# A gated delta-rule block with a 4-bit feed-forward: decay exponents from differences of running sums in bf16 pieces, filler products removed, steps reordered

## The reference

```python
gk = -jnp.exp(A_log) * jax.nn.softplus(hidden_states @ Wgk + dt_bias)
beta = jax.nn.sigmoid(hidden_states @ Wb + b_b)
def step(S, inp):
    qt, kt, vt, bt, gt = inp
    S = S * jnp.exp(gt)[..., None, None]
    kv = jnp.einsum('bhk,bhkv->bhv', kt, S)
    delta = (vt - kv) * bt[..., None]
    S = S + jnp.einsum('bhk,bhv->bhkv', kt, delta)
    ot = jnp.einsum('bhk,bhkv->bhv', qt, S)
    return (S, ot)
```

## Time and profile before

| what | value |
|---|---|
| time, median of 3 runs | 2731.93 us (2730.82 to 2735.35) |
| the profiled execution, its own time | 2730.7 us |
| its span | 2728.9 us |
| busy PE, DVE, ACT, POOL | 2608.6, 2389.7, 2259.6, 1628.3 us |
| mean granted clock of PE | 0.984 of full |

### The profile page before, as it was taken

The page is one execution under the profiler, slowest core; times in us unless marked ns, Lnnn a source line. Parts: engine busy times, 40 slices in busy tenths (PEclk is TensorE's granted clock), DMA queues, the critical chain, the costliest instruction groups (busy, mean ns, idle before and its releaser), DMA issues.

```text
span 2728.9 us, 73946 instructions
## 1 busy us (share of the span) xinstructions
PE 2608.6 (96%) x25743; PEld 2079.5 (76%) x25743; DVE 2389.7 (88%) x6753; ACT 2259.6 (83%) x7042; POOL 1628.3 (60%) x2418
## 2 busy tenths in 40 slices
PE   5699999999999999999999999999999999999987
PEld 3478777788777788777788777788777787777776
DVE  7788989888999888999889999889989889989872
ACT  4588888888888888888888888888888888888874
POOL 3565556665556665556665556665556665556660
PEclk8799999999999999999999999999999999999997
DMA  2111221111211111221111221202221201221201
GB/s 71 23 29 25 39 39 30 35 27 28 39 39 28 37 25 30 39 40 26 39 23 32 39 40 26 39 18 37 39 39 26 39 15 40 39 39 26 39 13 28
DMA packets 319616, 90.34 MB, mean 33 GB/s; under 512 B 283344, under 2 KB 310288, under 8 KB 319248
## 3 DMA queue, kind: packets, MB, share of 16 engines
q1 hardware_dynamic: 319248, 85.60, 16.3%
HBM read 46.77 MB, written 38.80 MB: 31 GB/s over the span
## 4 chain that ended last, share of the span: by engine, by line
PE 66%; DVE 25%; ACT 5%; issue 2%; POOL 1%; DMA 1%; SPq 0%; DVEq 0%; ACTq 0%; POOLq 0%
DVE KQ L862 13%; DVE vc L862 7%; PE bank_o L1279 6%; PE ring L1314 6%; PE ring L1171 6%; PE ring L1138 5%; PE bank_e L1249 4%; PE ring L1077 4%; PE bank_e L1261 3%; PE ring L1297 3%; PE bank_e L1256 3%; PE bank_o L1285 3%; PE bank_e L1265 3%; PE ring L1154 3%; PE ring L1183 3%; PE ring L1113 2%
## 5 line engine op out<-in xcount | busy, mean ns | idle before, releaser
L563 POOL TENSOR_TENSOR laneA<-laneA,laneT 96x30 f32<-96x30 f32 (+14 forms) x960 | 520.8, 542 | 75.2
L560 POOL TENSOR_TENSOR laneT<-laneA 96x30 f32<-96x30 f32 (+14 forms) x960 | 503.8, 525 | 68.0
L862 DVE SCALAR_TENSOR_TENSOR KQ<-ring,ckq,KQ 128x255 f32<-128x255 f32 (+2 forms) x1152 | 456.7, 470 | 49.8 <-ACT KQ L647 49.8
L862 DVE SCALAR_TENSOR_TENSOR vc<-ring,cvv,vc 128x255 f32<-128x255 f32 (+2 forms) x1152 | 462.1, 470 | 6.8 <-ACT vc L669 1.9
L542 POOL TENSOR_TENSOR gm<-g,mle 128x512 f32<-128x512 f32 x192 | 197.5, 1051 | 213.9 <-DVE UP L951 198.9
L951 DVE SCALAR_TENSOR_TENSOR UP<-ring,cj,gm 128x256 f32<-128x256 f32 x768 | 309.0, 475 | 1.7 <-PE ring L1138 0.2
L548 POOL TENSOR_TENSOR sqk<-sse,phalf 128x8 f32<-128x8 f32 x96 | 156.2, 1639 | 254.3 <-DVE sse L926 254.3
L761 ACT ACTIVATE junk<-V 128x128 f32<-128x128 f32 x768 | 231.9, 308 | 49.0 <-ACT V L735 25.8
L531 POOL TENSOR_TENSOR rstd<-veps,mhalf 128x2 f32<-128x2 f32 x32 | 23.0, 719 | 376.2 <-DVE veps L880 376.2
L686 ACT ACTIVATE V<-ring,sqk 128x128 f32<-128x128 f32 x768 | 219.2, 403 | 31.9 <-PE ring L1162 31.9
L1018 DVE SCALAR_TENSOR_TENSOR V<-V,rO,ring 128x128 f32<-128x128 f32 x768 | 211.4, 339 | 33.0 <-POOL rO L573 25.5
(11 more groups left out here) (162 smaller groups left out, 7874.4 us busy)
## 6 DMA issues: line engine op xcount, KB each, us to landing
to_lanes<-UP SPq DMA_DIRECT2D x128, 96.0 KB, 2.6
laneA<-to_lanes SPq DMA_DIRECT2D x32, 384.0 KB, 3.1
...
UP<-from_lanes SPq DMA_DIRECT2D x128, 96.0 KB, 3.3
...
```

The costliest lines, as they stand in the source:

```text
L560: link(nc.gpsimd.tensor_tensor(t, A[:, 0:m, j:j + 1].broadcast_to([LANES, m, n]), A[:, j:j + 1, j + 1:BLK].broadcast_to([LANES, m, n]), AL ...
L563: link(nc.gpsimd.tensor_tensor(w, w, t, ALU.add))
L862: ins = nc.vector.scalar_tensor_tensor(acc[:, n, s:T], src[:, n * T:n * T + T - s], wt(n)[:, TAPS - 1 - s:TAPS - s], acc[:, n, s:T], ALU.m ...
```

## The change

The exponent of a pair of tokens (i, j) was a sum over the tokens between them, by a product of 128 x 128 x 512 in fp32. It now is the difference of two running sums. `g` is rounded to a coarse grid (`gs` 1) with a remainder (`gs` 2); `GC` makes the running sums of both, and they are cut into three bf16 pieces each: ACT writes the first (`gp` 0), and the new DVE step `GS` the two others. The new PE step `GT` turns the pieces into rows, and ACT copies these into `gr`. `DD` is now a bf16 product of 512 columns with the mask, one of 512 columns with `ohn` (rows of minus one that pick a unit), and four of 128 columns with `ohp`. `DDg` and its 192 POOL instructions are gone, and `DDr` waits for what `DDg` waited for. The four `KW` are gone.

The order is new. `QK` 0 and `VP` 0 with their readers have moved to the end of the iteration before (offset 2), with their bank plan. `LANEP` 6 and 7 and the four DMA steps behind them have moved past the end of the iteration into the next one, and `STORE` and `FETCH` now stand ahead of `TSTORE` and `TFETCH`.

```diff
@@ pool
-                    if kind == "DDg":
...
-                        nc.gpsimd.tensor_tensor(out=decay(a), in0=bc(g[:, :, 2 * a:2 * a + 2].rearrange("p t h -> p h t"), 3, P),
-                                                in1=mle[:, :].unsqueeze(1).unsqueeze(1).broadcast_to([P, 2, NT, P]),
-                                                op=ALU.mult).then_inc(s_gm, 1)
@@ scalar
                     if kind == "GC":
                         nc.scalar.activation(eG2[:, par(), :], b[:, 0:NU], ACT.Exp)
-                        nc.scalar.activation(eR[:, :], b[:, NU:2 * NU], ACT.Exp).then_inc(read("GC", 0), 1)
+                        nc.scalar.activation(eR[:, :], b[:, 3 * NU:4 * NU], ACT.Exp)
+                        nc.scalar.activation(gp[:, :, 0, :, :], sums(b), ACT.Copy).then_inc(s_gp, 1)
+                    if kind == "GT":
+                        nc.scalar.activation(gr[:, :, :].rearrange("p f n -> p (f n)"), b[0:GR_ROWS, 0:2 * P],
+                                             ACT.Copy).then_inc(read("GT", 0), 1)
@@ vector
-                        link(nc.vector.tensor_tensor(g[:, :, :], zb[:, :, 0:NH], bc(negA[:, :], 1, NT), ALU.mult))
-                        dve.sem_inc(s_g, 1)
+                        link(nc.vector.tensor_tensor(gs[:, 0, :, :], zb[:, :, 0:NH], bc(negA[:, :], 1, NT), ALU.mult))
+                        link(nc.vector.tensor_scalar(gs[:, 1, :, :], gs[:, 0, :, :], grid[:, 0:1], grid[:, 0:1],
+                                                     ALU.add, ALU.subtract))
+                        nc.vector.tensor_tensor(gs[:, 2, :, :], gs[:, 0, :, :], gs[:, 1, :, :], ALU.subtract).then_inc(s_g, 1)
+                    if kind == "GS":
+                        b = bank("GC", 0)
+                        dve.wait_ge(s_gp, cnt(i, 1, 1))
+                        link(nc.vector.tensor_tensor(sums(b), sums(b), gp[:, :, 0, :, :], ALU.subtract))
+                        link(nc.vector.tensor_copy(gp[:, :, 1, :, :], sums(b)))
+                        nc.vector.tensor_tensor(gp[:, :, 2, :, :], sums(b), gp[:, :, 1, :, :], ALU.subtract)\
+                          .then_inc(read("GC", 0), 1)
@@ tensor
+                    if kind == "GT":
+                        b = take("GT", 0)
+                        pe.wait_ge(read("GC", 0), rv(i, "GC", 0))
+                        for f in range(2):
+                            ins = mm(b[0:GR_ROWS, f * P:(f + 1) * P], gp[:, f, :, :, :].rearrange("p k t h -> p (k t h)"),
+                                     identb[:, :], start=True, stop=True)
+                        ins.then_inc(full("GT", 0), 1)
                     if kind == "DD":
                         b = take("DD", a)
-                        pe.wait_ge(s_gm, cnt(i, NP, a + 1))
-
-                        mm(b[:, :], mgt[:, :], decay(a).rearrange("p h t n -> p (h t n)"), start=True, stop=False)
-                        mm(b[:, :], identb[:, :], negm[:, :, :].rearrange("p u n -> p (u n)"), start=False, stop=True)\
-                            .then_inc(full("DD", a), 1)
+                        mm(b[:, :], identb[:, :], negm[:, :, :].rearrange("p u n -> p (u n)"), start=True, stop=False)
+                        pe.wait_ge(read("GT", 0), rv(i, "GT", 0))
+                        f, q = a // 3, 4 * (a % 3)
+                        mm(b[:, :].rearrange("p (u n) -> p u n", u=4), gr[:, f, :], bc(ohn[:, q:q + 4], 2, P), start=False, stop=False)
+                        for u in range(4):
+                            ins = mm(b[:, u * P:(u + 1) * P], ohp[:, q + u:q + u + 1].broadcast_to([GR_ROWS, P]), gr[:, f, :], start=False, stop=(u == 3))
+                        ins.then_inc(full("DD", a), 1)
-                    if kind == "KW":
-
-                        if not zero(i):
-                            pe.wait_ge(s_or, cnt(i, len(O_SLOTS), 0))
-                        mm(BO[:, :], ident[:, :], wv[:, 0:4 * P], start=True, stop=True)
```

More of the change, by code:

```diff
@@ L21 @@
 NG = 3
+GR_ROWS = 3 * 2 * 2 * NP
 GH = NH // NG
@@ L30 @@
 ORDER = (
[L31 to L40, removed]
@@ L67 @@
[L67 to L70, removed]
+    ("QK", 1, 1), ("ZB", 0, 1), ("QKr", 1, 1), ("VT", 2, 0), ("QKt", 1, 1), ("ZBe", 0, 1), ("ZBg", 0, 1),
+    ("VT", 3, 0), ("VT", 4, 0), ("VTr", 2, 0), ("LANEP", 6, 0), ("QK", 2, 1), ("QKr", 2, 1), ("VTr", 4, 0),
@@ new lines @@
+    ("QK", 3, 1), ("QKr", 3, 1), ("LANEP", 7, 0), ("VTr", 3, 0), ("QKt", 2, 1), ("QKt", 3, 1), ("GC", 0, 1),
+    ("GCr", 0, 1), ("GS", 0, 1), ("VT", 5, 0), ("VTr", 5, 0), ("STORE", 0, 0), ("VP", 1, 1), ("VPr", 1, 1),
+    ("QT", 0, 1), ("VPt", 1, 1), ("TSTORE", 0, 0), ("QK", 4, 1), ("QTr", 0, 1), ("QKr", 4, 1), ("QKt", 4, 1),
+    ("FETCH", 0, 0), ("GT", 0, 1), ("GTr", 0, 1), ("QK", 5, 1), ("DD", 0, 1), ("VPs", 0, 1), ("QKr", 5, 1),
+    ("QKt", 5, 1), ("TFETCH", 0, 0), ("DD", 1, 1), ("QKs", 1, 1), ("QKs", 2, 1), ("QKs", 3, 1), ("VP", 2, 1),
@@ new lines @@
+    ("QT", 1, 1), ("VPr", 2, 1), ("DDr", 0, 1), ("DDr", 1, 1), ("QN", 0, 1), ("QTr", 1, 1), ("QT", 2, 1),
+    ("DD", 2, 1), ("QT", 3, 1), ("QTr", 2, 1), ("VPt", 2, 1), ("DDr", 2, 1), ("DD", 3, 1), ("QN", 1, 1),
+    ("MY", 0, 0), ("SSr", 0, 1), ("MYr", 0, 0), ("DDr", 3, 1), ("MY", 1, 0), ("QTr", 3, 1), ("QN", 2, 1),
+    ("MZ", 0, 0), ("MZr", 0, 0), ("MYr", 1, 0), ("GR", 0, 1), ("CJ", 0, 1), ("QN", 3, 1), ("GRr", 0, 1),
+    ("GR", 1, 1), ("GRr", 1, 1), ("GRr", 2, 1), ("GRr", 3, 1), ("XQ0", 0, 1), ("QKs", 4, 1), ("MY2", 0, 0),
[4 rows of a table added]
@@ new lines @@
+    ("MZ", 2, 0), ("DDr", 5, 1), ("CJ", 2, 1), ("GRr", 6, 1), ("MZr", 2, 0), ("GRr", 7, 1), ("GRr", 8, 1),
[4 rows of a table added]
+    ("SO", 9, 0), ("FU", 0, 1), ("FUr", 0, 1), ("LOUT", 0, 1), ("SQ", 9, 0), ("KTr", 0, 1), ("FUm", 0, 1),
[3 rows of a table added]
+    ("GPr", 0, 0), ("HQ", 1, 1), ("VPs", 2, 1), ("SE", 13, 0), ("GPr", 1, 0), ("SO", 13, 0), ("LANEP", 2, 1),
[10 rows of a table added]
+    ("OTr", 4, 0), ("VPr", 5, 1), ("VPr", 0, 2), ("HQ", 3, 1), ("HT", 0, 1), ("HT", 1, 1), ("OTr", 5, 0),
+    ("WO", 4, 0), ("VPt", 5, 1), ("WO", 5, 0), ("HTr", 0, 1), ("HTr", 1, 1), ("VPt", 0, 2), ("VPs", 5, 1),
@@ L71 @@
+    ("YOr", 0, 0), ("QKs", 0, 2),
 )
@@ L75, in steps_of_an_iteration @@
     return list(ORDER)
-RING = ("MY", "MZ", "MY2", "MX", "MZ2", "XN", "ZB", "GC", "DD", "QK", "QT", "GR", "KT", "VP", "VT", "GP", "XQ", "FU", "HT", "OT", "YO")
+RING = ("MY", "MZ", "MY2", "MX", "MZ2", "XN", "ZB", "GC", "GT", "DD", "QK", "QT", "GR", "KT", "VP", "VT", "GP", "XQ", "FU", "HT", "OT", "YO")
 TAKES = {"FU": 2, "MX": 2, "GR": 2}
 NRING = 6
-READER = {"ZB": "ZBg", "QK": "QKt", "VP": "VPt", "GP": "OG", ("FU", 1): "FUm"}
+READER = {"ZB": "ZBg", "GC": "GS", "QK": "QKt", "VP": "VPt", "GP": "OG", ("FU", 1): "FUm"}
 def reader_of(kind, a, j):
@@ L176, in build @@
         beta = sb("beta", [P, NT, NH])
-        g = sb("g", [P, NT, NH])
+        gs = sb("gs", [P, 3, NT, NH])
+        gp = sb("gp", [P, 2, 3, 2 * NT, NP], BF16)
+        gr = sb("gr", [GR_ROWS, 2, P], BF16)
+        pick = sb("pick", [GR_ROWS, NU // 2])
+        ohp = sb("ohp", [GR_ROWS, NU // 2], BF16)
+        ohn = sb("ohn", [GR_ROWS, NU // 2], BF16)
+        grid = sb("grid", [P, 1])
         eR = sb("eR", [P, NU])
@@ L500, in _ @@
                                     base=0, pattern=[[-1, P]], channel_multiplier=1)
-            nc.gpsimd.affine_select(out=mle[:, :], in_=ones[:, :], compare_op=ALU.is_ge, fill=0.0,
+            nc.gpsimd.affine_select(out=mle[:, :], in_=ones, compare_op=ALU.is_ge, fill=0.0,
                                     base=0, pattern=[[1, P]], channel_multiplier=-1)
-            nc.gpsimd.affine_select(out=mgt[:, :], in_=ones[:, :], compare_op=ALU.is_gt, fill=0.0,
+            nc.gpsimd.affine_select(out=mgt[:, :], in_=ones, compare_op=ALU.is_gt, fill=0.0,
                                     base=0, pattern=[[-1, P]], channel_multiplier=1)
@@ L637, in iteration @@
                         nc.scalar.activation(eG2[:, par(), :], b[:, 0:NU], ACT.Exp)
-                        nc.scalar.activation(eR[:, :], b[:, NU:2 * NU], ACT.Exp).then_inc(read("GC", 0), 1)
+                        nc.scalar.activation(eR[:, :], b[:, 3 * NU:4 * NU], ACT.Exp)
[3 more added lines that the diff above has]
+                                             ACT.Copy).then_inc(read("GT", 0), 1)
                     if kind == "DD":
+                        p, back = (a - 4, 0) if a >= 4 else (a + 2, 1)
+                        if not back or not zero(i):
+                            act.wait_ge(read("GR", p, 0), rv(i - back, "GR", p, 0))
+                            act.wait_ge(read("GR", p, 1), rv(i - back, "GR", p, 1))
                         nc.scalar.activation(decay(a).rearrange("p h t n -> p (h t n)"), b[:, :], ACT.Exp)\
@@ L906, in iteration @@
                         if a == 0:
-                            dve.wait_ge(read("GC", 0), rv(i, "GC", 0))
+                            dve.wait_ge(s_gp, cnt(i, 1, 1))
                         dve.wait_ge(s_sse, cnt(i, NG, a + 1))
@@ L1151, in iteration @@
```

(2 more changed lines are left out.)

39 lines of the change are left out of this document (19 added, 20 removed), and 42 rows, old and new, of the table ORDER.

## The result

The changed kernel takes 2776.41 us in the median of four runs (2765.51 to 2784.26), beside 2732.82 us for the kernel before on the same chip: a ratio of 1.0153, with a 95% interval of 1.0138 to 1.0168. It is slower by 1.5%, where I forecast 2702 us. The profiled execution took 2765.5 us, its span is 2763.7, and the mean granted clock of PE is 0.960, against 0.984 before.

The account below looks back on a forecast made before the run. PE bounds one piece of each iteration and DVE the other: 21.5 + 58.1 + 1.4 = 81.0 us for 81.96, 30 us less over 31 distances, giving 2702 us. Likeliest case 2680 to 2725, whole range 2615 to 2785.

Parts of the forecast that it names:

- `DD`: Exponent product on PE: 0.88 us instead of 1.08; two of six stand in PE's piece, giving -0.4 us an iteration.
- the fillers: The four unread `KW` products, where PE waits anyway: removing them was worth nothing in the sum, apart from the clock.
- DVE's piece: Part from `QKt` 0 (newly `QKt` 1) to the next first `GRr`, bound by DVE: 24.57 us to become 21.5.
- PE's piece: Part from the first `GRr` to the last `WO`, chain nearly all on PE: 55.64 us to become 58.1.
- the wait of `GR` 2: In PE's piece, for banks that the third and fourth `GRr` free: 0 to 1.0 us, taken as 0.5.
- Between: From the last `WO` to DVE's piece: DVE's lag of 1.0 us plus `YOr` 0.4, so 1.4 us for 1.75.
- DVE idle ahead of `QKt` 1: Sign of being right: DVE's 1.32 us of idling between the pieces go, leaving none ahead of `QKt` 1.
- PE idle in DVE's piece: Sign of being right: PE idle some 5 us an iteration in the part that DVE bounds.
- Better balance: Rival: PE's piece does not grow and DVE bounds the loop at 79 us an iteration, 2635 us; chance 0.20.
- late fetch: Rival: `N` lands too late for `MY` 0, beyond 1.5 us of slack; chance 0.08, shared with DVE late at `SO`.
- The trade: Rival that it cancels: `GR` 2's wait and `DD`'s upper cost eat the gain, 2731 us, no change; chance 0.14.
- the clock rival: PE's clock falls in DVE's piece without fillers, between `QK` 3 and `GT`: 1 to 3.5 us an iteration; chance 0.22.

Follow-up runs that it names:

- the order alone: Kernel before with the new order, keeping POOL's `DDg` and the fp32 `DD`, without fillers, `GS` or `GT`: 2752.4 us, ratio 1.0066.
- the exponents alone: Kernel before with the new exponents (`GS`, `GT`, bf16 `DD`) in the old order, its four fillers kept: 2787.1 us, ratio 1.0191.

## Why the prediction was wrong, point by point

**The failed step: the fillers.** I wrote that they "are worth nothing in the sum: the taps cover them" and made the clock a rival of 0.22. Covered they are, in time (the undisturbed distance is 81.3 us with them and without); but in the changed kernel they were worth 65 us (2776.4 to 2711.3) by the clock, where in the kernel before they were worth 6. The mechanism of that rival came true, and its size was right: 58.3 / 29 = 2.0 us an iteration on average, inside my 1 to 3.5. That it eats the gain from 0.96 us on held too. Its worked price was mis-summed, though: at 2.5 us an iteration the 81.0 become 83.5 and the time 2702 + 31 x 2.5, some 2780 us, not the 2750 that I wrote. The place was wrong. I put it "between `QK` 3 and `GT`", the longest gap, and most of it hidden. Filling this gap changed nothing; what decides among the gaps of DVE's piece lies behind `DD` 0, where PE has three small gaps (0.40, 0.59 and 1.25 us), the last of which ends exactly where PE takes over the chain. The clock falls as `DD` 2 begins, and is met by work that is needed at once. I had named that work ("`DD` 2 to `GR` 1 ... needed at once"), with 5.5 us that would become up to 11; it was 3.85 that became 6.05, and 1.8 behind it.

**The likelihood.** What I should have weighed more is that three causes removed PE's work from the same stretch, and the earlier trace rows showed the consequence. The runs show that two of them are needed together: no fillers with the long `DD` brings one fall, the short `DD` with the four fillers none or one, both 18 or 22.

**`DD`.** Forecast 0.88, bounded by 0.66 and 1.32. It is 0.39 + 0.22 + 0.22 in the chain, of which 0.17 is the start behind the wait: 0.66, the lower end. The group of weight loads of the small products in the changed kernel:

```profile
L1147 PEld LDWEIGHTS ring<-gr,ohp 72*128 72x128 bf16 x768 | 65.6, 106 | 54.8 <-issue 15.8
```

Each load takes 106 ns as a record, but four products advance the chain by 0.22 us, 55 ns each. So a load of its own for each does not slow them down; my choice of 0.11, after the turnings of `OT`, was wrong. The Trainium skill, "TensorE: Matmul & The Clock Gate", section "Back-to-back issue gap", gives about 81 ns for such a pair in a sustained stream; the runs of four in this trace do not agree, and the rows decide.

**DVE's piece.** Forecast 21.5 us. From `QKt` 1 (843.03) to the first `GRr` (864.66) it is 21.63. The `gs` of line 912 takes 0.39 where I had 0.2, `GS` 0.56 for 0.6, and the taps are the count that I gave. But the chain leaves it at 859.45, so that four `DD`, not two, lie on PE's path.

**PE's piece.** Forecast 58.1. From 864.66 to the end of the last `WO`, at about 922.0 (its matmul ends are modelled), it is 57.3. PE idles for 0.41 us in all between 863.30 and 923.80, so the wait of `GR` 2, for which I took 0.5, did not come, and the two `DD` gave 0.84 where I had 0.4; the two make up the difference.

**Between.** Forecast 1.4: DVE 1.0 behind the last `WO`, and `YOr`. It is 2.4, with DVE 1.7 behind. The chain there runs over DVE, as forecast, while PE has only `QK` 1 and `ZB` to do.

The sum, 21.63 + 57.3 + 2.4 = 81.33, was forecast as 81.0: three terms off by 0.1, -0.8 and 1.0.

**DVE idle ahead of `QKt` 1**: 0.24 us, forecast none. **PE idle in DVE's piece**: 16.99 - 11.71 = 5.3 us, forecast some 5. **POOL**: its 43.7 us an iteration for 50.6 gave nothing to anyone, as forecast.

**The other rivals.** Better balance did not come: an undisturbed iteration has PE and DVE both in the chain for long stretches. No late fetch: `MY` 0 starts at 861.45 directly behind `DD` 3. The trade did not cancel, -0.6 to -0.8 us an iteration (81.33 for 81.94, or for the mean of 82.1), and the kernel with one filler gets it: 2712 us, faster than the kernel before and the changed one.

**The skill's second rule.** I let the clock rival rest on the Trainium skill's Part 4 in the same page, that turnings do not count as busy in the same way. The rival held, but not by that rule: eight turnings of the filler's length ended the series of falls as the filler did, and a quarter of a filler did too. So the run does not agree that turnings do not count; how much they count for is open. Part 1, that activity releases the clock, agrees with the trace: the clock came back at 1036.5 us behind 10.2 us in which PE was never idle.

**What stays open.** What makes the first fall of a series is not settled, nor what carries a series on, nor why a product in PE's piece removes most falls, nor whether less than a quarter of a filler would do. That the bank plan costs the order alone its 0.91 us, and the exponents alone their 0.83, was read from the chains and the plan; no run gave either kernel another bank.
